# An earlier list of looked-up experts and an earlier first pair, in a vision tower on one Trainium2 core

## What is computed

```python
# first mixture (8 experts, hidden 512, one expert for each token)
route = softmax(x @ router_w + router_b);  max_ind = argmax(route);  max_prob = max(route)
for e in range(8):
    oe = silu(xe @ w1[e]) * (xe @ w2[e]) @ w3[e]
    out = out + where(max_ind == e, oe, 0.0)
out = out.astype(bfloat16) * max_prob
# second mixture (8 experts, hidden 768, two experts for each token)
top_logits, top_idx = top_k(x @ router_w.T, 2);  top_w = softmax(top_logits)
for e in range(8):
    h = silu(x @ Wg[e].T) * (x @ Wu[e].T)
    out = out + h @ Wd[e].T * sum(top_w * (top_idx == e))
```

## Time and profile before

| | us |
|---|---|
| three timed runs | 378.39, 382.37, 384.23 |
| their median | 382.37 |
| the profiled execution | 379.88 |
| its span, first to last instruction | 378.2 |
| mean granted TensorE clock | 0.941 |
| TensorE matmul busy | 331.0 |
| VectorE, ScalarE, GpSimd busy | 190.6, 136.9, 89.1 |

### The profile page before, as it was taken

The page is one execution under the profiler, slowest core; times in us unless marked ns, Lnnn a source line. Parts: engine busy times, 40 slices in busy tenths (PEclk is TensorE's granted clock), DMA queues, the critical chain, the costliest instruction groups (busy, mean ns, idle before and its releaser), DMA issues.

```text
span 378.2 us, 6885 instructions
## 1 busy us (share of the span) xinstructions
PE 331.0 (88%) x2601; PEld 259.6 (69%) x2601; DVE 190.6 (50%) x513; ACT 136.9 (36%) x276; POOL 89.1 (24%) x120
## 2 busy tenths in 40 slices
PE   3999978878785995889988799869799999999996
PEld 1999964567662552354566475757699999999995
DVE  2785698684762441138696762458121612422125
ACT  2999220864223221132594233240321212222230
POOL 4199707000004322102005002001333332321110
PEclk9999996965989998799898999998999999999999
DMA  7944307996079999671006999020269999999623
GB/s 224 387 85 103 62 7 235 246 243 158 0 219 241 269 271 270 178 181 39 0 1 163 276 247 252 2 71 3 69 168 285 255 268 247 253 252 260 173 58 93
DMA packets 32050, 64.41 MB, mean 170 GB/s; under 512 B 10897, under 2 KB 17298, under 8 KB 32018
## 3 DMA queue, kind: packets, MB, share of 16 engines
q1 hardware_dynamic: 30098, 59.43, 60.5%
q0 software_dynamic: 1920, 4.56, 4.6%
HBM read 59.31 MB, written 4.65 MB: 169 GB/s over the span
## 4 chain that ended last, share of the span: by engine, by line
PE 61%; DVE 17%; DMA 6%; ACT 6%; issue 5%; SPq 3%; DVEq 0%
PE ps L1745 11%; PE ps L1770 9%; PE ps L1494 9%; PE ps L1757 6%; PE ps L1486 3%; DVE cv L1399 3%; DMA wdn<-in_m_w 3%; PE ps L1553 2%; DMA xg<-token_x,src_id 2%; PE ps L1829 2%; PE ps L1688 2%; PE ps L1862 2%; DMA xw<-in_xw 2%; PE ps L1608 1%; PE ps L1559 1%
## 5 line engine op out<-in xcount | busy, mean ns | idle before, releaser
L632 POOL DMA_INDIRECT xg<-token_x,src_id x22 | 21.4, 972 | 125.5 <-DVE src_id L1253 81.9
L1286 DVE TENSOR_TENSOR ht<-sg,ps 128x384 f32<-128x384 f32 (+1 forms) x48 | 23.6, 508 | 47.1 <-ACT sg L841 45.3
L1745 PE MATMUL ps<-xgt,wup 128*128 128x128 f32 x384 | 45.6, 275 | 1.2 <-DVE ht L1286 1.2
L1745 PEld LDWEIGHTS ps<-xgt,wup 128*128 128x128 f32 x384 | 44.8, 192 | 1.4 <-issue 1.4
L1494 PE MATMUL ps<-weff,xp 128*128 128x193 f32 x240 | 41.5, 336 | 1.3 <-ACT xp L691 1.3
L1494 PEld LDWEIGHTS ps<-weff,xp 128*128 128x128 f32 x240 | 40.9, 196 | 2.2 <-issue 2.2
L841 ACT ACTIVATE sg<-ps 128x384 f32<-128x384 f32 (+1 forms) x48 | 20.8, 454 | 47.5 <-PE ps L1757 27.5
L1486 PE MATMUL ps<-busy 128*128 128x512 bf16 x96 | 32.3, 451 | 4.5 <-POOL ident L542 4.5
L1770 PE MATMUL ps<-wdn,ht 128*128 128x192 f32 x192 | 35.2, 334 | 0.0
L639 POOL DMA_INDIRECT token_y<-ysb,row_id x20 | 19.7, 987 | 62.3 <-ACT ysb L848 62.3
L1770 PEld LDWEIGHTS ps<-wdn,ht 128*128 128x128 f32 x192 | 30.8, 190 | 1.8
(11 more groups left out here) (337 smaller groups left out, 588.8 us busy)
## 6 DMA issues: line engine op xcount, KB each, us to landing
wup<-in_m_w SPq DMA_DIRECT2D x16, 576.0 KB, 9.2
wup<-in_m_w SPq DMA_DIRECT2D x48, 192.0 KB, 9.8
wdn<-in_m_w SPq DMA_DIRECT2D x16, 576.0 KB, 12.1
wup<-in_m_w SPq DMA_DIRECT2D x14, 384.0 KB, 7.8
wup<-in_m_w SPq DMA_DIRECT2D x42, 128.0 KB, 8.1
wdn<-in_m_w SPq DMA_DIRECT2D x14, 384.0 KB, 10.7
xw<-in_xw SPq DMA_DIRECT2D x2, 784.0 KB, 11.6
wall<-in_w_sh SPq DMA_DIRECT2D x2, 768.0 KB, 9.8
```

The source lines that it names most:

```text
L632: g.indirect_dma_start(xg[:, j, :], None, token_x[m], bass.IndirectOffsetOnAxis(ap=src_id[:, j:j + 1], axis=0))\
L1286: v.tensor_tensor(ht[:, j % 2, s, 0:half], sg[:, s, 0:half], ups, ALU.mult)\
L1745: mm(ps[:, 2 * s + g, c * P:c * P + P], up[:, col:col + P], xgt[:, 0, j * P:j * P + P], start=(c == 0), stop=False)
```

## The change

It has two parts.

The three VectorE instructions that make `te` are moved from behind the gates to right behind the scan that makes `base_e`. This code is shared, so it happens in both mixtures. All that follows on VectorE (`rank_b`, `over_b`, `pick`, `slotf`, `one_first`, ...) stands behind them.

```diff
@@ scalar, experts(m)
                 for j in range(n):
                     if j == 0:
+                        if m == 0:
+                            silu(0, 0)
+                            silu(0, 1)
                         gathered(1)
...
-                    silu(j, 0)
-                    silu(j, 1)
+                    if (m, j) != (0, 0):
+                        silu(j, 0)
+                        silu(j, 1)
@@ vector, experts(m), behind the scan of base_e
+                link(v.tensor_tensor(teb[:, 0:over, :], base_e[0:1, 1:E].unsqueeze(1).broadcast_to([1, over, E - 1]),
+                                     iota_t[:, 0:over, :], ALU.is_le))
+                link(v.tensor_reduce(tef[:, 0:over], teb[:, 0:over, :], AX.X, ALU.add))
+                v.tensor_scalar(te[:, 0:over], tef[:, 0:over], float(E - 1), None, ALU.min).then_inc(S["v_te"], 1)
@@ vector, experts(m), behind the gates: the same three instructions go
@@ vector, the loop over the units
-                    if m == 0 and j >= 1:
+                    if m == 0 and j >= 2:
                         hidden_across(j - 1)
                     if j == 0:
+                        if m == 0:
+                            product(0, 0)
+                            product(0, 1)
+                            hidden_across(0)
                         gathered(1)
...
-                    product(j, 0)
-                    product(j, 1)
+                    if (m, j) != (0, 0):
+                        product(j, 0)
+                        product(j, 1)
@@ tensor, experts(0)
                     for j in range(n):
                         up_pair(j)
-                        if j >= 1:
+                        if j == 0:
+                            up_pair_rest(0)
+                            hidden_across(0)
+                            gathered(1)
+                            continue
+                        if j >= 2:
                             hidden_across(j - 1)
-                        if j == 0:
-                            gathered(1)
-                        elif j % 2 == 1 and j + 1 < n:
+                        if j % 2 == 1 and j + 1 < n:
                             gathered(j // 2 + 2)
...
                         up_pair_rest(j)
-                        if j >= 1:
-                            down_pair(j - 1)
+                        down_pair(j - 1)
```

More of the change, by code:

```diff
@@ L1266, in experts @@
                     link(v.tensor_tensor(gate[:, 1], gate[:, 0], ex8[:, :, 0], ALU.mult))
[L1268 to L1271, removed]
                 def gathered(i):
```

## The result

The changed kernel takes 386.32 us (median of 20 runs, 383.18 to 390.13), the kernel before 380.76 us (20 runs, 375.31 to 384.66). The ratio is 1.0212, with a 95% interval of 1.0178 to 1.0247; it leaves disturbed runs out, which is why it lies above the ratio of the two medians, 1.015. The forecast was 382.6 us, no change beyond noise, with a range of 378.4 to 385.8. The kernel became slower, by 5.6 us in its medians and by some 8 us by the ratio (0.0212 × 380).

A forecast was written before the change was run, and what follows sets the result against it. The prediction took weight transfer to bound the first mixture and the entry to count in the second; −0.4 + 0.6 + 0 = +0.2 us on the median of 382.37 gave 382.6 us, range 378.4 to 385.8.

The forecast's parts named there:

- The bound: First mixture: transfer of the weights binds, not TensorE or SyncE's issuing; DMA busy share 1.04 from 119 to 157 us.
- The first mixture's terms: First mixture: −0.4 us (0 to −0.8) from making `te` early, 0 from pair 0 ahead of the gathered rows.
- The step that failed: First mixture, halves 9 and 10: DMA engines have work until about 130.4 us, half 10 under way by 128.4, no gap.
- my latest time: First mixture: `down_pair(0)` done at 127.6 us at the latest, with the gathers late.
- The gathers: First mixture, beside half 8's packets: gathers stay near 5 to 7 us; up to 6.7 us taken for tile 1's.
- The clock: Rival, second mixture's entry: TensorE's clock rises later, `first_tile` up to 4.4 us instead of 2.71; about 385.4 us, 13%.
- my 126.3 to 127.6: First mixture: end of `down_pair(0)` in us, depending on the gathers, against 126.99 before.
- The list's price on VectorE: Three instructions making `te`, now ahead of `slotf` and `one_first`: 0.62 us, between 0.47 and 0.84.
- The second mixture's +0.6 us: Second mixture's entry: the moved instructions are all on the path, 0.5 to 0.85 us slower.
- The list's gain: First mixture: half 8's first load leaves 3.6 us earlier, but the stream gains only 0.4 us (0 to 0.8).
- Pair 0's order: First mixture, pair 0 ahead of the gathered rows: off the path, 0, with +1 at the bound if gathers come late.
- the held-up gathers: Rival, first mixture: 3 us more on each gather, DMA engines run dry; +2.2 us in all, 384.6 us, 12%.

The follow-up runs named there:

- te_idle: Changed kernel with `down_pair(0)` ahead of `gathered(1)`, `te` made where VectorE waits for `sources` (first mixture) or late as before (second): 380.86 us, ratio 1.000 to before.
- order_alone: Kernel before with only pair 0's new order, `te` (the list) made late as before: 381.01 us, ratio 1.005 to before.
- down_early: Changed kernel with `down_pair(0)` moved ahead of `gathered(1)`: 383.09 us, ratio 1.008 to the kernel before.

## Why the prediction was wrong

**The bound.** That the first mixture is bound by the transfer of weights was right: the four kernels with 3.5 us of standstill or more are also the four slowest. The first mixture's terms summed to −0.4 us, and it lost 5.2.

**The step that failed** is this one: "It matters only if the engines run dry first. Half 9's last byte landed at 124.2 + 6.6 = 130.8, about 130.4 in the new order, and half 10 would be under way by 128.4 at the latest. No gap." The engines ran dry at 126.1, and half 10's first load left at 132.49. Both times were off by some 4 us, and in opposite directions.

*Dry at 126.1, not 130.4.* A landing time isn't the end of the engines' work. After, half 9's last load lands at 118.2 + 9.5 = 127.7, with nothing issued behind it by SyncE, and the engines' share is down to 0.14 from 126 us on and 0.02 from 127. The row of that load, issue and time to landing:

```profile
L449 SPq DMA_DIRECT2D yg<-in_m_w x1: 448/448/448, 118.2 to 118.2; - x1
...
DMA to landing us min/median/max: 9.5/9.5/9.5
```

By the bytes, before would have been through 1.7 to 2.2 us behind 127.72, at some 129.7 and not 130.8 (an estimate). Then the early list filled the engines better than I had counted: 266 GB/s from 103.5 to 126.1 against 252 before, worth some 1.2 us where I took 0.4. And the stream began 2.0 us earlier in this execution (103.5 against 105.5), though the code ahead of it is unchanged. Of the 2.5 us by which I let `down_pair(0)` be late (129.5 against 126.99), some 2 were there in the execution that I read; in one whose stream begins 1.6 us further ahead of the scan, hardly any would be (an estimate).

*Half 10 at 132.49, not 128.4.* `down_pair(0)` came 4 us beyond my latest time, by the gather and by the clock.

**The gathers.** I bounded tile 1's gather by the traced 4.2 to 6.7 us (the 4.2 is a weight load's; the gathers in these rows took 5.1 to 6.7), but in the rows tile 1's gather had been issued ahead of half 8. With half 8 (five loads, 1.18 MB) issued 1 to 4 us ahead of it, it took 7.9 to 9.1 us in seven kernels; with half 8 leaving 1 to 2.2 us behind it, 3.5 to 5.4 us in five. The rule of the Trainium skill ("DMA: Bandwidth & Descriptors", section Queues, rings and completion order), that an engine goes round its queues, isn't refuted by that, but my reading of it, that the gathers would stay near 5 to 7 us, is: the measurement decides. Whether the turn of a large load's packets or something else makes up the 3 to 4 us wasn't tried.

**The clock.** I had pair 1's products at 1.94 us and they took 3.68. TensorE's short work between 118 and 123 us in place of one pause didn't hold the clock. I had weighed the clock only in the second mixture, where it did nothing: `first_tile` took 2.69 us against 2.71.

`down_pair(0)` ended at 131.7, 5.4 us behind the earlier end of my 126.3 to 127.6: 3.0 us by pair 1's later start (124.27 against 121.3), 1.7 us by its slower products, the rest by transposes and rest products at the lower clock.

**What held.** The list's price on VectorE: 0.53 us in the second mixture, 0.55 in the first, against 0.62. The second mixture's +0.6 us, of which 0.5 stand in the trace. Half 8's first load left at 112.2 where I had 113.3. The list's gain is at best my 0.4 us, by te_idle not measurable. Pair 0's order by itself is worth nothing measurable, by order_alone.

**The rival that came true** is the one of the held-up gathers, to which I gave 12%. Its chain of events was the right one; I let the standstill begin at 130.3 us where it began at 126.1, and left the clock out of it. So it came to +2.2 us, and the measured medians say +5.6.

## What to carry to other kernels

A load that was issued earlier while the engines were full gained nothing here, and what was issued behind it, a small gather that TensorE waits for, came later. How long the transfer engines can do without the next load is read from the bytes that they still have to move (all that was issued, less what has been moved since the stream began), not from the last landing. And when a stream hangs on one release, take that release out from behind whatever can be late: `down_pair(0)` needed no gathered row, and moved ahead of the wait it closed the gap.

## What the runs showed of the hardware that was not expected

- One indirect gather of 128 rows: 3.5 to 5.4 us to landing where it was issued ahead of a 1.18 MB set of loads, 7.9 to 9.1 us where the set had begun 1 to 4 us earlier.
- At a full share the DMA engines moved 263 GB/s over the whole stream in before and 248 in down_early, with the same bytes: 3 us from one execution to another (50.8 against 53.7 us). What sets this rate is open.
- A load's landing can stand well behind the point at which the engines have little left to do: in after, half 9's last load landed at 127.7 us, and the engines' share was 0.14 from 126 us on and 0.02 from 127.
- The unchanged part between the mixtures took 84.9 or 88.3 us with a granted clock of 0.96 or 0.92 (before and after).
